# Two graph layers on one core: SP's loads of x, first weights and filters moved, the last two tiles' roots from POOL to VectorE

## What is computed

```
x = layernorm(x + relu(segment_sum(xp[src] * norm, dst) + xp * self_norm + b)),   xp = x @ W
x = layernorm(x + L1(x)),  with
    sj, vj  = (x[:, :C] @ Win_s)[idx_j], (x[:, C:] as (C, 3) @ Win_v)[idx_j]
    W       = (shifted_softplus(f_ij @ Wf1 + bf1) @ Wf2 + bf2) * rcut
    agg     = segment_sum(products of sj, vj, the unit vector of r_ij, and W)
    S, V    = agg_s @ W1_s -> shifted_softplus -> @ W2_s;   agg_v @ W1_v @ W2_v
```

## Time and profile before

| | |
|---|---|
| median of 3 runs | 1068.62 us (1068.15 to 1070.77) |
| the profiled execution | 1060.5 us, its span 1058.7 us |
| busy share of the span | PE 89%, DVE 79%, ACT 66%, POOL 61% |
| DMA | 280.43 MB, mean 265 GB/s |
| SP's queue, share of 16 engines | 49.3% |
| POOL's queue, share of 16 engines | 40.6% |
| largest lines of the chain | PE L1309 14%, POOL L610 11%, PE L1313 7% |

### The profile page before, as it was taken

The page is one execution under the profiler, slowest core; times in us unless marked ns, Lnnn a source line. Parts: engine busy times, 40 slices in busy tenths (PEclk is TensorE's granted clock), DMA queues, the critical chain, the costliest instruction groups (busy, mean ns, idle before and its releaser), DMA issues.

```text
span 1058.7 us, 17988 instructions
## 1 busy us (share of the span) xinstructions
PE 945.2 (89%) x5218; PEld 770.2 (73%) x5218; DVE 834.9 (79%) x2358; ACT 702.8 (66%) x1641; POOL 645.9 (61%) x945
## 2 busy tenths in 40 slices
PE   7889888999983999999999479999999999928885
PEld 6768777777762888888888358878888888818774
DVE  7688888886833889888888568888888888808997
ACT  4569877777771466666666446666666666518997
POOL 4028888888861466666666444676667765534665
PEclk9989999998996999999999789999999999969997
DMA  9989999999999499989998677999999999768998
GB/s 346 418 285 245 247 240 240 240 246 237 244 213 282 156 324 336 338 320 320 334 329 321 241 243 177 224 214 208 218 228 217 206 217 214 112 125 342 412 401 334
DMA packets 105702, 280.43 MB, mean 265 GB/s; under 512 B 13106, under 2 KB 17478, under 8 KB 105606
## 3 DMA queue, kind: packets, MB, share of 16 engines
q1 hardware_dynamic: 68598, 191.42, 49.3%
q0 software_dynamic: 35280, 82.63, 40.6%
q10 hardware_dynamic: 1728, 5.24, 1.3%
HBM read 132.38 MB, written 146.87 MB: 264 GB/s over the span
## 4 chain that ended last, share of the span: by engine, by line
PE 26%; POOL 23%; issue 14%; DMA 13%; DVE 2%; ACT 2%; SPq 0%; POOLq 0%; DVEq 0%; ACTq 0%
PE bank L1309 14%; POOL sum L610 11%; PE bank L1313 7%; POOL G_mem L596 6%; DMA sum<-R_mem,l_sidx 4%; POOL sum L549 4%; PE bank L1300 3%; DMA sum<-R_mem,sidx_all 3%; DMA out<-edge_mem 2%; POOL G_mem L533 2%; DMA out<-R_mem 1%; DVE stat L1161 1%; DMA out<-G_mem 1%; DMA edge_mem<-sum 1%; POOL node_mem L533 1%
## 5 line engine op out<-in xcount | busy, mean ns | idle before, releaser
L549 POOL DMA_INDIRECT sum<-R_mem,sidx_all x79 | 128.2, 1623 | 84.9 <-DMA sum<-zeros 48.8
L610 POOL DMA_INDIRECT sum<-R_mem,l_sidx x79 | 135.9, 1720 | 46.3 <-issue 21.9
L596 POOL DMA_INDIRECT G_mem<-x_d,dst_i x79 | 77.2, 978 | 90.7 <-PE bank L1344 66.0
L1309 PE MATMUL bank<-G_hi 128*128 128x512 f32 x316 | 130.4, 413 | 0.0
L1309 PE MATMUL bank<-G_lo,G_hi 128*128 128x512 f32 x316 | 124.2, 393 | 0.0
L1223 PE MATMUL bank<-G_hi,M_mem 128*128 128x512 f32 x200 | 86.1, 431 | 7.0 <-ACT R_mem L682 5.3
L1313 PE MATMUL bank<-G_hi,G_lo 128*128 128x512 f32 x316 | 85.3, 392 | 0.0
L1113 DVE SCALAR_TENSOR_TENSOR edge_mem<-edge_mem,Y,bank 128x128 f32<-128x128 f32 x237 | 71.3, 385 | 15.0 <-ACT edge_mem L803 15.0
L1340 PE MATMUL bank<-edge_mem,Winv 128*128 128x512 f32 x158 | 81.8, 600 | 0.1
L1223 PE MATMUL bank<-G_lo,M_mem 128*128 128x512 f32 x200 | 80.5, 403 | 0.0
L1234 PE MATMUL bank<-edge_mem,Wf_s 128*128 128x256 f32 x320 | 79.3, 392 | 0.7 <-ACT node_mem L676 0.7
(11 more groups left out here) (258 smaller groups left out, 2922.1 us busy)
## 6 DMA issues: line engine op xcount, KB each, us to landing
node_mem<-sum SPq DMA_DIRECT2D x41, 512.0 KB, 5.9
filt_d<-node_mem SPq DMA_DIRECT2D x40, 512.0 KB, 5.0
node_mem<-filt_d SPq DMA_DIRECT2D x79, 256.0 KB, 4.9
sum<-zeros SPq DMA_DIRECT2D x33, 512.0 KB, 14.2
G_mem<-x SPq DMA_DIRECT2D x20, 512.0 KB, 6.4
x_d<-node_mem SPq DMA_DIRECT2D x20, 512.0 KB, 2.9
sum<-node_mem SPq DMA_DIRECT2D x20, 512.0 KB, 4.3
edge_mem<-x SPq DMA_DIRECT2D x19, 512.0 KB, 6.4
```

The source lines that it names most:

```text
L549: pool.indirect_dma_start(sum0, bass.IndirectOffsetOnAxis(ap=sidx[:, t:t + 1], axis=0), R[t % 8][:, :], None, compute_op=ALU.add).then_inc ...
L596: pool.indirect_dma_start(G3[t % 8][:, :], None, x1_d, bass.IndirectOffsetOnAxis(ap=dst_i[:, t:t + 1], axis=0)) \
L610: pool.indirect_dma_start(sum1, bass.IndirectOffsetOnAxis(ap=l1_sidx[0:n, t:t + 1], axis=0), R3[t % 8][0:n, :], None, compute_op=ALU.add). ...
L1309: pe.matmul(bank[4 + a][:, :], zT_hi[a][:, c * P:(c + 1) * P], w[c][:, :], start=(c == 0 and w is W0h), stop=False)
```

## The change

Four moves, all in the order of instructions:

- Of the four pairs of x that SP loads in the seam, only the first stays ahead of the wait for the scatters. Pairs 1 to 3 are loaded in `nodes0`, each in front of its pair of sums.
- The four loads of `W0` stand behind the zero fill at the start, ahead of the second pair of filter inputs.
- SP waits for the first gather of the second edge loop before it loads filters 1 to 3 and index rows 1 to 3.
- The ladders of the last two pairs of the last stage are done by DVE, in five operations, with a signal of their own (`g_root`); ACT and DVE wait for that instead of `g_rstd`, and POOL's loop ends two pairs earlier.

```diff
@@ SP
             sp_.dma_start(sum0[41 * 256:, :], zeros[:, 0:D]).then_inc(s_zero0, 16)
+            for c in range(4):
+                sp_.dma_start(W0_s[c], W0[c * P:(c + 1) * P, :]).then_inc(s_wres, 16)
...
-            for c in range(4):
-                sp_.dma_start(W0_s[c], W0[c * P:(c + 1) * P, :]).then_inc(s_wres, 16)
             sp_.wait_ge(e_lo, T)
...
-            for j in range(4):
-                x_in(j)
+            x_in(0)
             for k in range(4):
                 sp_.wait_ge(w_st[k], 16 * (T // 8))
             sp_.wait_ge(e_scat, 16 * TR)
...
             def nodes0(j):
                 if j < T2:
+                    if 1 <= j < 4:
+                        x_in(j)
                     wait(sp_, n_tr, 2 * j - 6)
...
             for j in range(T2 + 6):
                 nodes0(j)
+            sp_.wait_ge(f_gather[0], 16)
             for t in range(1, 4):
                 filt_in(t)
                 trow_in(t)
@@ POOL
-            for t in range(T2):
+            for t in range(T2 - 2):
@@ ACT, nodes1
-                    act.wait_ge(g_rstd, K_ROOT * (t + 1))
+                    if t < T2 - 2:
+                        act.wait_ge(g_rstd, K_ROOT * (t + 1))
+                    else:
+                        act.wait_ge(g_root, K_RSTD * (t - T2 + 3))
@@ DVE, nodes1
-                    dve.wait_ge(g_rstd, K_ROOT * (t6 + 1))
+                    if t6 < T2 - 2:
+                        dve.wait_ge(g_rstd, K_ROOT * (t6 + 1))
...
+                if s - 5 in (T2 - 2, T2 - 1):
+                    t5 = s - 5
+                    w, m5 = tiny4[t5 % 4], mv4[t5 % 4]
+                    root = Stage(g_root, t5 - T2 + 2, K_RSTD)
+                    dve.tensor_scalar(w[:, 0, :], m5[:, :, 1], EPS, None, ALU.add)
+                    dve.wait_ge(g_rs, 2 * (t5 + 1))
+                    root.mark(dve.scalar_tensor_tensor(w[:, 3, :], w[:, 2, :], -0.5, w[:, 2, :], ALU.mult, ALU.mult))
+                    root.settle(dve)
+                    root.mark(dve.tensor_tensor(w[:, 4, :], w[:, 3, :], w[:, 0, :], ALU.mult))
+                    root.settle(dve)
+                    root.mark(dve.scalar_tensor_tensor(w[:, 5, :], w[:, 4, :], 1.5, w[:, 2, :], ALU.add, ALU.mult))
+                    root.settle(dve)
+                    root.mark(dve.scalar_tensor_tensor(w[:, 6, :], m5[:, :, 0], -1.0, w[:, 5, :], ALU.mult, ALU.mult))
+                    root.settle(dve)
```

More of the change, by code:

```diff
@@ L374, in build @@
         g_rstd = sem("g_rstd")
+        g_root = sem("g_root")
         g_y0 = sem("g_y0")
```

## The result

| | before | after |
|---|---|---|
| median | 1068.74 us (1068.15 to 1070.77, 4 runs) | 1061.16 us (1060.66 to 1062.35, 4 runs) |
| ratio | | 0.9932, 95% interval 0.9917 to 0.9947 |
| profiled execution, span | 1060.5, 1058.7 us | 1060.8, 1058.7 us |

The time is 7.3 us less by the ratio (interval 5.7 to 8.9), against 6.1 forecast. But the two profiled executions are equal. The prediction took the kernel before to be 0.8% slower in its runs than in its profile for no stated reason. The traces give one, and it bears on how much of the 7.3 us belongs to the change.

A forecast was written before the change was run, and what follows sets the result against it. Transfers bound the first edge loop, TensorE the node stage and second edge loop. Gains 3.0 - 0.2 + 2.2 + 1.1 = 6.1 us took the profiled 1060.5 to 1054.4; with the 0.8% carried over, 1062.5 us, range 1057.8 to 1068.0.

The forecast's parts named there:

- I carry the difference over unchanged: Whole kernel: median of the runs, 1068.62 us, is 0.8% above the profiled 1060.5; the same was assumed after the change.
- Part B: Start, weights behind the zero fill: costs 0.2 us through a later filter input, bounds 0 and 2.5.
- lands by 72.2, and TensorE takes it at 71.96: First loop's start: the filter input behind 1 MB of weights lands at most 2.5 us later, costing 0.2 us.
- Rival 1: Start: weights are served beside the zero fill's tail, POOL's start at 69.93 moves by up to 2.5 us; chance 0.10.
- Part A: Seam before the node stage: last scatter lands 4.4 us earlier, third tile 1.4 later; gain 3.0 us, between 1.2 and 5.2.
- each half alone would win little: Seam before the node stage: without the early weights the casts would still wait until some 324 or later.
- Rival 2: Seam before the node stage: scatters are slow by themselves, 4.4 us not won, the change gives 1.7 (1066.9); chance 0.12.
- Rival 3: Seam before the node stage: TensorE's clock falls in the wait for the second pair, 2.4 us lost (1064.9); chance 0.08.
- Part C: Seam before the second edge loop: filters held until the first gather lands; gain 2.2 us, bounds 0.5 and 2.8.
- The 0.8 us of the stores: Seam before the second edge loop: the last two x1 stores, without filters beside them, return 0.8 us.
- Part D: Tail: the last two tiles' ladder on VectorE instead of POOL; gain 1.1 us, bounds 0.5 and 1.3.
- Rival 4: First loop: shifted filter input gives a longer rhythm, 0.6 us in each of 17 groups, 10 us lost (1072.5); chance 0.05.

The follow-up runs named there:

- late x: Only three of the four pairs of x moved behind the last scatters, weights left in their old place, against the kernel before: 1067.14 us, ratio 0.9986.
- the wait for the gather: Only SP's wait for the first gather before filters 1 to 3, added to the kernel before: 1067.09 us, ratio 0.9981.
- x ahead: The change with all four x loads ahead of the last scatters: 1058.76 us, 0.9975 of before; with weights behind the filter inputs too: 1053.76 us, 0.9954.

## Why the prediction was right or wrong

**The time** (1062.5 in 1057.8 to 1068.0; 1061.16 measured) and the direction came out. That the gain came so near, 7.3 for 6.1, is in part luck: one step had no reason, one part had a wrong price that the stop hides, and on two other chips the same change gained 1.5 and 2.2 us by the ratios.

**"I carry the difference over unchanged".** This step had no mechanism. The profile of before is an execution without the stop, its timed runs were about 8 us longer, and the runs of the chip where all four profiles have the stop have the same median, 1068.43. Some 6 to 7 of the 8 us are then the stop, as the first filter matmul shows (50.83, and 57.0 to 58.1 with it). No profile of the kernel before itself has it, so this rests on the kernel whose start is identical. A part's worth had to be asked for twice, with and without the stop.

**Part B, 0.2 us: wrong where there is no stop, about 3.5 us there.** The step that failed is "lands by 72.2, and TensorE takes it at 71.96". The filter input came at 73.0 to 73.4 in the four profiles, about 1 us later than 1 MB at 410 GB/s gives from the earlier trace rows. TensorE was ready for it before 71.96: at 70.3 to 71.3 in these four, and it took it at 70.5 and 71.2 in two other profiles without early weights; that of the kernel before was at a granted clock of 0.50 from 64 to 70 us, and late. And the sum left out the clock behind the wait, which took the cost over the bound of 2.5 us. With the stop the whole chain of compute is 6 us late and the filter input is there in time: the second group starts at 88.5 (late x) and 90.8 (the wait for the gather) without early weights, and at 88.4, 90.4 and 91.2 with them. The spread is as large without them, so the rows show no cost of the weights there.

**Rival 1, the weights delay the zero fill: refuted**, by 69.88 beside 69.91. The rule of the Trainium skill (DMA: Bandwidth & Descriptors, Queues, rings and completion order), that a semaphore write waits only for earlier writes, agrees with this; the conclusion drawn from it, that the part would then cost at most 0.2 us, does not hold, as the loads queued behind the weights come late.

**Part A, 3.0 us: right in direction, about 1.9 measured, and loosely.** From the last scatter's start to the first big matmul it was 15.5, 15.9, 12.4 and 16.9 us in the four profiles with the seam in its old order, and is 12.9 to 13.8 in the six with both moves (means 15.2 and 13.5). From the last scatter of the group before, which takes the wait between the groups in, it was 24.6 to 29.0 and is 24.1 to 25.2 (means 26.7 and 24.7). The last scatter took 9.6, 9.0, 6.6 and 10.9 us and takes 5.2 to 5.8, so the 9.62 of the sum was no fixed price. In the kernel after the landing gave 3.9 instead of 4.4 (5.75 us, not 5.2), and the second pair cost 1.7 instead of 1.4 (7.6 us behind the scatter for 5.9; 7.6 to 8.3 over the six). That each half alone would win little was wrong for the weights: alone they won 3.3 us on the first chip, since 2 MB of x without them does not slow the scatter much (5.8, 5.8 and 6.8 us in three profiles). The casts started at 324.7 and not at 318.3, since the filters had moved with the loop; the scatter still covered them. **Rival 2, scatters slow by themselves**, is refuted by the 5.2 to 5.8.

**Rival 3, the clock: wrong at its place**, as the matmuls from 346.72 on are at full speed and neither the transposes ahead of the wait nor the wait brought the granted clock down, **and right elsewhere**: the loss that it describes, a wait and then the same work at half speed, happened at 74 us behind the filter input.

**Part C, 2.2 us: 1.8 measured.** The gather's 1.4 became 1.8 (4.97 us to the first transposes, before 6.78). The 0.8 us of the stores was not won: from their issue to the first gather it is 4.88 us now and was 4.90.

**Part D, 1.1 us: as predicted**, 1.0 to 1.2 in the traces.

**Rival 4, a longer rhythm: not seen.** From the second group to the last scatter of the first loop it is 241.9 to 244.9 us in thirteen of the fourteen profiles, whatever the kernel (242.2 and 243.4 in the two of the kernel before), and 246.0 in the one left, with x ahead.

The sum without the stop is 1.9 - 3.5 + 1.8 + 1.1 = 1.3 us, beside 1.5 and 2.2 measured with an interval of about 1.5 each way. With the stop and a free Part B it would be 4.8; measured were 7.3, with 5.7 the lower end of the interval. The parts timed on the first chip, both moves of the seam and the wait for the gather, gained 2.0 and 2.0 by the ratios, and with the tail's 1.1 that is 5.1. The 2 us that are missing from 7.3 are no more than the intervals of these three measurements leave open (each about 1.5 us each way). They are not explained, and whether they are real is not known: the whole change was not run on the first chip.

## What to carry to other kernels

Cost a moved load for everything behind it on its queue, not only for the signal ahead of it: a small input behind 1 MB comes when that megabyte is through, and what it then costs is its lateness and the clock behind the wait. Put such a load behind the small inputs that the next stage waits for, not ahead of them; here that returned 2.4 us. Take the base of such a sum from more than one profile: the seam's slow scatter was 6.6 us in one execution and 10.9 in another. And where a profile and the timed runs differ by more than the runs do among themselves, look for the reason before adding up small gains: a gain can be hidden by it, or exist only with it.

## What the runs showed of the hardware that was not expected

- The stop: from about 15 to 24 us all compute engines fall nearly idle with "issue" as the main cause, in five of fourteen profiles: in that of the kernel after, in four of four on the first chip of the experiments, in none of eight on two others, and not in that of the kernel before. TensorE is busy 2.2 to 2.9 of the 8 us from 16 to 24, and all 8 without it. The share of the DMA engines is the same with and without it (1.01 to 1.11 from 16 to 24 us, in windows of 2 us), so their load alone does not decide it. It costs 6 to 7 us at the first filter matmul.
- An SP issue of 256 KB takes 1.4 us while the engines are saturated by the transfers ahead (5.55 us for four), and one of 40 KB there 1.3 us (2.57 for two); at 340 us, right behind the last scatter, SP issues a load of 512 KB in 0.43 us.
- A wait of 3.07 us of TensorE at a granted clock of 1.00 was followed by 6.7 us at 0.56. In the four profiles with this wait (1.67 to 3.07 us) the clock fell 0.7 to 2.7 us behind its end, not in it.
